# Causal attention with a quantized feed-forward: accumulators of P·V per slot, one score bank per slot, and softmax steps in another order on VectorE

## The chip, the cores and the metric

The kernel runs on all 8 cores of one Trainium2 chip, the same program on each with data of its own; the cores exchange nothing. Cores 2b and 2b+1 share batch item b and split its query tiles between them. The time is that of the slowest core in microseconds (us), from device counters. Lower is better.

## The reference

The input `x` is 4 x 4096 x 1024. With `xn = layernorm(x)`:

```python
q, k, v = xn @ Wq.T, xn @ Wk.T, xn @ Wv.T
qk   = (q @ k.T) * C ** (-0.5)          # C = 1024, so 1/32
attn = softmax(where(causal, qk, -inf))
out  = x + attn @ v + (xn @ quantize_int4(kernel) + bias + (xn @ a) @ b)
```

## The kernel before

Every instruction goes through `Plan.op(engine, function, waits, inc)`. The plan keeps one list for each engine, T (TensorE), V (VectorE), S (ScalarE), Y (SyncE, which issues DMAs) and G (GpSimd, which issues DMAs), in the order in which the Python code calls it, and each list is replayed as that engine's queue. So the order of the code is the order of the work: an instruction whose semaphores are not there yet holds up all that stands behind it in its own queue and nothing else. There is no scheduler.

**Stage 1** (to about 460 us) computes K (transposed, to memory) and V (kept in SBUF as `v_res`, bf16) for all 4096 tokens of the batch item, and quantizes the feed-forward weights on VectorE beside it. **Stage 2a** (to about 610 us) computes Q and the feed-forward for the core's own 2048 rows and writes both to memory. The Q projection `e_qproj` accumulates 8 matmuls into one of two banks `psQ`, and ScalarE evicts each bank to `qstage` (L607).

**Stage 2b** (from 631 us) is attention. The 2048 rows are 16 slots of 128 rows. Slot `si` in processing order sees `kcap = 256 * (16 - si)` keys, from 4096 down to 256. Slots go in pairs `k` of an even slot A (`a = 0`) and an odd slot B (`a = 1`). The parts are:

- `e_scores(k)`: the keys come in chunks of 512. For each chunk first A and then B gets a group of 8 matmuls (L809) into a PSUM bank `psS[a][ci % 2]`, two banks for each slot of the pair and four in all. VectorE casts the bank to bf16 `scores` (L821) and takes the maximum of the chunk into `mxcols` (L827, the last chunk after a mask is added, L831 and L835). The next group of the same bank waits for the cast (`sc_prev`). K chunks beyond the first 1024 keys come through a ring of three buffers `kbuf`.
- `e_softmax(si)`: VectorE takes the maximum over the chunks into `mxv` (L855) and scales it by -1/32 into `nbias` (L859). ScalarE takes the exponentials of the row in two halves (L867, L870) with a scale of 1/32, that bias, and row sums into `lsum`. VectorE adds the two sums (L873) and takes the reciprocal into `invl` (L876). `mxv`, `nbias` and `lsum` are single tiles for all slots, so the maximum of B waits for the reciprocal of A.
- `e_trans_av(si)`: for each block of 128 keys a transpose of the probabilities into `psT` (L894), a copy to `ptb` by ScalarE (L900), and two matmuls (L909) into `psAV[0]` and `psAV[1]`, the halves of the 1024 output columns. The transposes run one block ahead. There is one such accumulator; the first matmul of a slot waits for the epilogue of the slot before (`epi_V[si - 1]`).
- `e_epilogue(si)`: VectorE multiplies both halves by `invl` and adds the feed-forward (L928, L931), then adds `x` (L935), and GpSimd's queue stores the result (L940). `e_sdma_fx` loads the feed-forward and `x` tiles, `e_sdma_qt` the query tiles (L755).

The order is written out at the end: after `e_scores(0)`, for each `k`: softmax A, softmax B, scores of pair `k + 1`, product and epilogue of A, product and epilogue of B.

Of the kernel before, what the change touches and what calls it, by code (L numbers as in the profile page):

```python
# [118 lines left out]
def build_nc():  # L119
# [556 lines left out]
    def sb3(n, s, t):  # L676
        return p2b.enter_context(nc.sbuf_tensor(n, s, t))
# [94 lines left out]
    def e_scores(k):  # L772
# [8 lines left out]
        for ci, (off, wdt) in enumerate(chunks):  # L781
# [6 lines left out]
            for a, (jx, kcx, mx_prev) in enumerate(  # L788
# [5 lines left out]
                for dc in range(NCH):  # L794
                    w = []
                    if dc == 0:
                        w.append(v)
                        prev = sc_prev.get((a, ci % 2))
                        if prev is not None:
                            w.append(prev)  # L800
                        if ci == 0:
                            w.append(qt_dma[si])
# [6 lines left out]
                    P.op("T", lambda e, si=si, a=a, ci=ci, dc=dc, wdx=wdx, kap=kap: e.matmul(  # L809
                        psS[a][ci % 2][:, 0:wdx],  # L810
# [8 lines left out]
                if ci == 0 and k >= 2:  # L819
                    wev.append(exp_S.get(2 * (k - 2) + a))  # L820
                ev = P.op("V", lambda e, kp=kp, a=a, ci=ci, off=off, wdx=wdx: e.tensor_copy(  # L821
                    out=scores[kp][a][:, off:off + wdx], in_=psS[a][ci % 2][:, 0:wdx]),
                    waits=wev, inc=chV)
                sc_prev[(a, ci % 2)] = ev
# [25 lines left out]
    def e_softmax(si):  # L850
        a = si % 2
        j = ORDER[si]
        kcap = slot_kcap(j)
        nch = len(score_chunks(kcap))
        v1 = P.op("V", lambda e, a=a, nch=nch: e.reduce_max(  # L855
            mxv[:, :], mxcols[a][:, 0:nch], axis=AX.X),
            waits=[sc_mx_V[si], inv_V.get(si - 1)], inc=chV)
        mx_fin[si] = v1
        v2 = P.op("V", lambda e: e.tensor_scalar(  # L859
            out=nbias[:, :], in0=mxv[:, :], scalar1=-SCALE, scalar2=None, op0=ALU.mult),  # L860
            waits=[v1], inc=chV)
        w = [v2, exp_S.get(si - 1)]
        if si >= 2:
# [5 lines left out]
            bias=nbias[:, 0:1], scale=SCALE, accum_out=lsum[:, 0:1]), waits=w, inc=chS)  # L869
        exp_S[si] = P.op("S", lambda e, kp=kp, a=a, half=half, kcap=kcap: e.activation(  # L870
            out=pbuf[a][:, half:kcap], in_=scores[kp][a][:, half:kcap], func=AF.Exp,
            bias=nbias[:, 0:1], scale=SCALE, accum_out=lsum[:, 1:2]), inc=chS)
# [3 lines left out]
        inv_V[si] = P.op("V", lambda e, si=si: e.reciprocal(  # L876
            out=invl[si % 2][:, :], in_=lsum[:, 0:1]),
            waits=[vsum, epi_V.get(si - 2)], inc=chV)

    def e_trans_av(si):  # L880
# [23 lines left out]
        def em_av(kc):  # L904
            for h in range(2):
                w2 = [ptb_ev[kc]]
                if kc == 0 and h == 0 and si >= 1:
                    w2.append(epi_V.get(si - 1))
                av_lastk[kc] = P.op("T", lambda e, kc=kc, h=h, nk=nk: e.matmul(  # L909
                    psAV[h][:, :], ptb[kc % 3][:, :],  # L910
                    v_res[:, kc * C + h * 512: kc * C + (h + 1) * 512],
                    start=(kc == 0), stop=(kc == nk - 1), skip_group_check=True),
                    waits=w2, inc=chT)
# [9 lines left out]
    def e_epilogue(si):  # L923
        j = ORDER[si]
        w = [av_T[si], inv_V[si], ff_dma[si], xr_dma[si]]
        if si >= 2:
            w.append(out_G[si - 2])
        P.op("V", lambda e, si=si: e.scalar_tensor_tensor(  # L928
            out=outsb[si % 2][:, 0:512], in0=psAV[0][:, :], scalar=invl[si % 2][:, 0:1],
            in1=fftile[si % 3][:, 0:512], op0=ALU.mult, op1=ALU.add), waits=w, inc=chV)  # L930
        v2 = P.op("V", lambda e, si=si: e.scalar_tensor_tensor(  # L931
            out=outsb[si % 2][:, 512:1024], in0=psAV[1][:, :], scalar=invl[si % 2][:, 0:1],
# [124 lines left out]
```

How the kernel before makes its waits and increments, by code:

```python
    def replay(self, eng, engobj, sems):  # L102
        for ws, fn, semname, amt in self.items[eng]:
            seen = set()
            for n, v in ws:
                key = n
                if key in seen:
                    v = max(v, dict(ws).get(n, v))
                    continue
                seen.add(key)
                vv = max(val for (nn, val) in ws if nn == n)
                engobj.wait_ge(sems[n], vv)
            ins = fn(engobj)
            if semname is not None:
                ins.then_inc(sems[semname], amt)
```

## Time and profile before

| | us |
|---|---|
| median of 2 runs | 1031.19 (1031.08 to 1031.31) |
| the profiled execution's own time | 1031.55 |
| span of its slowest core (core 2), first to last instruction | 1030.0 |
| spans of the eight cores | 1016.6 to 1030.0 |
| TensorE matmuls busy, of the span | 754.1 (73%) |
| VectorE busy | 473.7 (46%) |
| ScalarE busy | 271.7 (26%) |
| mean granted TensorE clock of core 2, share of full speed | 0.887 |

Busy shares are means over stages with different limits. The profile also gives for each instruction its start, its duration and what it waited for; "idle before" is the time that its engine stood still just before it, with the instruction that ended the wait. Some matmul records are missing from a trace (a few per cent). The granted clock is 1.00 at 2.4 GHz and 0.50 at 1.2 GHz, and a value between is a mean over a stretch.

### The profile page before, as it was taken

What the parts mean: (1) busy time and instruction counts of PE and PEld (TensorE: products, weight loads), DVE (VectorE), ACT (ScalarE), POOL (GpSimd) and SP (SyncE); (2) the same over time, 40 slices, a digit from 0 to 9 for tenths busy, and PEclk for the clock granted to TensorE, in tenths of its full rate; (3) what the DMA queues carried; (4) which work ended last, traced back from release to release, by engine and by line L of the source; (5) the groups of instructions that cost most, each with busy time, mean ns of one, the idle gap of its engine ahead of it and who ended that gap; (6) DMA issues with size and microseconds to landing.
All of it is one profiled execution on the core that took longest, in us unless ns stands there. A gap on an engine that the chain in (4) does not pass through costs nothing.

```text
span 1030.0 us, 12140 instructions; the slowest of 8 cores (1016.6 to 1030.0 us)
## 1 busy us (share of the span) xinstructions
PE 754.1 (73%) x3129; PEld 319.7 (31%) x3191; DVE 473.7 (46%) x798; ACT 271.7 (26%) x617; POOL 41.0 (4%) x70
## 2 busy tenths in 40 slices
PE   0055988998998995157989764698878787788752
PEld 0001333343333442012434332344434343333320
DVE  1236467686685695063363322661161331522442
ACT  0023333433333331123121100113413324233321
POOL 2000000000000001000000000000001001011110
PEclk9997999899999998578989886899988898888985
DMA  8970031422403102920421239743243043033232
GB/s 178 215 102 1 41 54 49 103 28 76 102 11 92 56 7 80 158 34 41 122 84 82 82 127 302 266 131 115 102 167 120 21 164 124 21 123 121 82 133 95
DMA packets 35316, 103.32 MB, mean 100 GB/s; under 512 B 2706, under 2 KB 15252, under 8 KB 30772
## 3 DMA queue, kind: packets, MB, share of 16 engines
q0 software_dynamic: 22720, 44.11, 19.9%
q1 hardware_dynamic: 12532, 58.43, 15.7%
q8 instruction: 31, 0.51, 0.2%
q14 instruction: 33, 0.27, 0.1%
HBM read 92.11 MB, written 29.36 MB: 118 GB/s over the span
## 4 chain that ended last, share of the span: by engine, by line
PE 56%; DVE 16%; issue 12%; DMA 9%; ACT 5%; DVEq 1%; SPq 0%; ACTq 0%; POOLq 0%; POOL 0%
PE psAV L909 15%; PE psK L366 9%; PE psS L809 9%; PE psV L393 5%; PE psQ L601 5%; PE psF L631 4%; DMA w<-wker 4%; DMA xga<-xcols 2%; DMA qtile<-qT_h 2%; PE psT L894 2%; ACT pbuf L867 1%; ACT pbuf L870 1%; DVE outsb L935 1%; DVE outsb L928 1%; DVE xg L346 1%
## 5 line engine op out<-in xcount | busy, mean ns | idle before, releaser
L909 PE MATMUL psAV<-v_res,ptb 128*128 128x512 bf16 x527 | 161.4, 411 | 45.7 <-DVE outsb L935 25.4
L393 PE MATMUL psV<-wvb,xg 128*128 128x512 bf16 x504 | 115.8, 387 | 14.4 <-ACT v_res L403 14.0
L900 ACT COPY ptb<-psT 128x128 bf16<-128x128 bf16 x272 | 70.4, 265 | 198.6 <-PE psT L894 196.4
L366 PE MATMUL psK<-xg,wkb 128*128 128x512 bf16 x497 | 113.0, 383 | 5.3 <-ACT kst L372 2.9
L809 PE MATMUL psS<-kbuf,qtile 128*128 128x512 bf16 (+1 forms) x330 | 78.6, 402 | 21.2 <-DVE scores L821 20.9
L909 PEld LDWEIGHTS psAV<-v_res,ptb 128*128 128x128 bf16 x544 | 53.6, 102 | 117.1 <-issue 98.2
L928 DVE SCALAR_TENSOR_TENSOR outsb<-psAV,invl,fft 128x512 f32<-128x512 f32 x16 | 12.0, 750 | 162.9 <-PE psT L894 71.5
L809 PE MATMUL psS<-k_res,qtile 128*128 128x512 bf16 (+1 forms) x236 | 55.9, 396 | 30.0 <-DMA qtile<-qT_h 29.7
L393 PEld LDWEIGHTS psV<-wvb,xg 128*128 128x128 bf16 x512 | 50.3, 99 | 78.8 <-issue 23.8
L366 PEld LDWEIGHTS psK<-xg,wkb 128*128 128x128 bf16 x512 | 50.3, 99 | 66.7 <-issue 8.0
L894 PE MATMUL psT<-identb_s,pbuf 128*128 128x128 bf16 x272 | 59.8, 230 | 6.6 <-ACT pbuf L867 6.4
L631 PE MATMUL psF<-weff,xga 128*128 128x512 bf16 x251 | 58.8, 391 | 7.9 <-DVE ffst L645 7.5
L821 DVE CAST scores<-psS 128x512 bf16<-128x512 f32 x72 | 47.4, 658 | 33.8 <-PE psS L809 33.4
L601 PE MATMUL psQ<-xga,wqb 128*128 128x512 bf16 x249 | 57.5, 387 | 3.6 <-ACT qst L607 2.9
L372 ACT CAST kst<-psK 128x512 bf16<-128x512 f32 x64 | 37.3, 585 | 69.5 <-PE psK L366 69.5
L809 PEld LDWEIGHTS psS<-kbuf,qtile 128*128 128x128 bf16 x336 | 35.3, 106 | 65.3 <-issue 35.6
L288 ACT ACTIVATE sq<-xg 128x512 bf16<-128x512 bf16 x64 | 38.5, 626 | 40.6 <-PE T L298 38.6
L530 PE MATMUL U<-xga,onescol_s 128*1 128x512 bf16 x32 | 16.7, 523 | 43.1 <-ACT sqa L524 32.9
L867 ACT ACTIVATE pbuf<-scores,nbias 128x2048 bf16<-128x2048 bf16 (+15 forms) x16 | 19.2, 1201 | 108.4 <-DVE nbias L859 90.9
L809 PEld LDWEIGHTS psS<-k_res,qtile 128*128 128x128 bf16 x240 | 24.0, 102 | 61.4 <-issue 39.0
L294 PE MATMUL T<-xg,onescol_s 128*1 128x512 bf16 x64 | 32.8, 512 | 12.7 <-DVE rbc_s L334 11.1
L827 DVE TENSOR_REDUCE mxcols<-scores 128x1 f32<-128x512 bf16 x56 | 38.4, 686 | 5.8
(102 smaller groups left out, 755.1 us busy)
## 6 DMA issues: line engine op xcount, KB each, us to landing
kbuf<-kT_h SPq DMA_DIRECT2D x21, 1024.0 KB, 6.7
w<-wker SPq DMA_DIRECT2D x16, 512.0 KB, 6.9
xg<-xfm POOLq DMA_DIRECT2D x8, 1024.0 KB, 11.7
kT_h<-kst SPq DMA_DIRECT2D x8, 1024.0 KB, 3.8
ff_h<-ffst SPq DMA_DIRECT2D x16, 512.0 KB, 2.7
fft<-ff_h POOLq DMA_DIRECT2D x16, 512.0 KB, 6.2
xrt<-xrows POOLq DMA_DIRECT2D x16, 512.0 KB, 7.2
out<-outsb POOLq DMA_DIRECT2D x16, 512.0 KB, 2.9
```

Source lines behind the costliest of these rows:

```text
L288: sq_S[(g, cc)] = P.op("S", lambda e, g=g, cc=cc: e.activation(out=sqb[cc % 2][:, :], in_=xg[g % 3][:, cc * G1:(cc + 1) * G1], func=AF.Squ ...
L366: P.op("T", lambda e, g=g, dc=dc, cc=cc: e.matmul(psK[dc % 2][:, :], wkb[:, :].rearrange("p (a x) -> p a x", a=NCH)[:, cc, dc * 128:(dc + ...
L372: ev[dc] = P.op("S", lambda e, g=g, dc=dc: e.copy(out=kstage[g % 2][:, dc * G1:(dc + 1) * G1], in_=psK[dc % 2][:, :]), waits=[tmm] + ([kst ...
L393: P.op("T", lambda e, g=g, tt=tt, h=h, cc=cc: e.matmul(psV[tt % 2][h][:, :], xg[g % 3][:, cc * G1 + tt * 128: cc * G1 + (tt + 1) * 128], w ...
L601: P.op("T", lambda e, b=b, dc=dc, cc=cc: e.matmul(psQ[dc % 2][:, :], wqb[:, :].rearrange("p (a x) -> p a x", a=NCH)[:, cc, dc * 128:(dc + ...
L631: P.op("T", lambda e, b=b, tt=tt, h=h, cc=cc: e.matmul(psF[tt % 2][h][:, :], xga[b % 3][:, cc * G1 + tt * 128: cc * G1 + (tt + 1) * 128], ...
L809: P.op("T", lambda e, si=si, a=a, ci=ci, dc=dc, wdx=wdx, kap=kap: e.matmul(psS[a][ci % 2][:, 0:wdx], qtile[si % 4][:, dc * 128:(dc + 1) * ...
L821: ev = P.op("V", lambda e, kp=kp, a=a, ci=ci, off=off, wdx=wdx: e.tensor_copy(out=scores[kp][a][:, off:off + wdx], in_=psS[a][ci % 2][:, 0 ...
L827: P.op("V", lambda e, kp=kp, a=a, ci=ci, off=off, wdx=wdx: e.reduce_max(mxcols[a][:, ci:ci + 1], scores[kp][a][:, off:off + wdx], axis=AX. ...
L894: tt = P.op("T", lambda e, a=a, kc=kc: e.transpose(psT_[kc % 2][:, :], pbuf[a][:, kc * 128:(kc + 1) * 128], identb[:, :]), waits=w, inc=chT)
L900: ptb_ev[kc] = P.op("S", lambda e, kc=kc: e.copy(out=ptb[kc % 3][:, :], in_=psT_[kc % 2][:, :]), waits=wv, inc=chS)
L909: av_lastk[kc] = P.op("T", lambda e, kc=kc, h=h, nk=nk: e.matmul(psAV[h][:, :], ptb[kc % 3][:, :], v_res[:, kc * C + h * 512: kc * C + (h ...
```

## The change

The change touches four things.

1. The 16 halves of PSUM used in stage 2b are dealt out anew: `psAV` becomes two accumulators of two banks, chosen by the parity of the slot, and `psS` becomes one bank for each slot of a pair instead of two. The first P·V matmul of a slot waits for the epilogue of the slot two before, and each score group waits for the cast of the group before it in the same slot.
2. `e_softmax` is split. `e_sm_pre` has the maximum and the exponentials, `e_sm_post` the sum and the reciprocal. The scores of the next pair now stand between the two.
3. The factor 1/32 moves from the softmax to the eviction of Q. The maximum is taken with its sign changed, straight into `nbias`, and the separate scaling on VectorE is gone. The maximum of B waits for the exponentials of A, because `nbias` is still one tile.
4. `lsum` has two columns for each slot of a pair.

```diff
-            ev[dc] = P.op("S", lambda e, b=b, dc=dc: e.copy(
+            ev[dc] = P.op("S", lambda e, b=b, dc=dc: e.activation(
                 out=qstage[b % 2][:, :].rearrange(
                     "p (o a t) -> p o a t", o=4, a=NCH)[:, :, dc, :],
-                in_=psQ[dc % 2][:, :].rearrange("p (o t) -> p o t", o=4)),
+                in_=psQ[dc % 2][:, :].rearrange("p (o t) -> p o t", o=4),
+                func=AF.Copy, scale=SCALE),
...
-    lsum = sb3("lsum", [128, 2], F32)
+    lsum = sb3("lsum", [128, 4], F32)
...
-    psS = [[ps3(f"psS{a}_{i}", [128, 512]) for i in range(2)] for a in range(2)]
+    psS = [ps3(f"psS{a}", [128, 512]) for a in range(2)]
     psT_ = [ps3(f"psT{i}", [128, 128], BF16) for i in range(2)]
-    psAV = [ps3(f"psAV_{h}", [128, 512]) for h in range(2)]
+    psAV = [[ps3(f"psAV{i}_{h}", [128, 512]) for h in range(2)] for i in range(2)]
...
-                        prev = sc_prev.get((a, ci % 2))
+                        prev = sc_prev.get(a)
...
-                sc_prev[(a, ci % 2)] = ev
+                sc_prev[a] = ev
...
-    def e_softmax(si):
+    def e_sm_pre(si):
...
         v1 = P.op("V", lambda e, a=a, nch=nch: e.reduce_max(
-            mxv[:, :], mxcols[a][:, 0:nch], axis=AX.X),
-            waits=[sc_mx_V[si], inv_V.get(si - 1)], inc=chV)
+            nbias[:, :], mxcols[a][:, 0:nch], axis=AX.X, negate=True),
+            waits=[sc_mx_V[si], exp_S.get(si - 1)], inc=chV)
         mx_fin[si] = v1
-        v2 = P.op("V", lambda e: e.tensor_scalar(
-            out=nbias[:, :], in0=mxv[:, :], scalar1=-SCALE, scalar2=None, op0=ALU.mult),
-            waits=[v1], inc=chV)
-        w = [v2, exp_S.get(si - 1)]
+        w = [v1, exp_S.get(si - 1)]
...
-            bias=nbias[:, 0:1], scale=SCALE, accum_out=lsum[:, 0:1]), waits=w, inc=chS)
+            bias=nbias[:, 0:1], scale=1.0, accum_out=lsum[:, 2 * a:2 * a + 1]), waits=w, inc=chS)
...
-        vsum = P.op("V", lambda e: e.tensor_tensor(
-            out=lsum[:, 0:1], in0=lsum[:, 0:1], in1=lsum[:, 1:2], op=ALU.add),
+
+    def e_sm_post(si):
+        a = si % 2
+        vsum = P.op("V", lambda e, a=a: e.tensor_tensor(
+            out=lsum[:, 2 * a:2 * a + 1], in0=lsum[:, 2 * a:2 * a + 1],
+            in1=lsum[:, 2 * a + 1:2 * a + 2], op=ALU.add),
             waits=[exp_S[si], inv_V.get(si - 1)], inc=chV)
...
-                if kc == 0 and h == 0 and si >= 1:
-                    w2.append(epi_V.get(si - 1))
+                if kc == 0 and h == 0 and si >= 2:
+                    w2.append(epi_V.get(si - 2))
...
-                    psAV[h][:, :], ptb[kc % 3][:, :],
+                    psAV[si % 2][h][:, :], ptb[kc % 3][:, :],
...
     for k in range(NP2):
-        e_softmax(2 * k)
-        e_softmax(2 * k + 1)
+        e_sm_pre(2 * k)
+        e_sm_pre(2 * k + 1)
         if k + 1 < NP2:
             e_sdma_qt(k + 1)
             e_scores(k + 1)
+        e_sm_post(2 * k)
+        e_sm_post(2 * k + 1)
```

On VectorE, in the cycle of pair 1, from the last epilogue of pair 0 to the first casts of the scores of pair 2, before the change (`psS0_0` is the first bank of the even slot, `psS0_1` its second):

```order
L935 TENSOR_TENSOR outsb1<-outsb1,xrt1 128x1024
L855 TENSOR_REDUCE mxv<-mxcols0 128x1
L859 TENSOR_SCALAR nbias<-mxv 128x1
L873 TENSOR_TENSOR lsum<-lsum 128x1
L876 RECIPROCAL invl0<-lsum 128x1
L855 TENSOR_REDUCE mxv<-mxcols1 128x1
L859 TENSOR_SCALAR nbias<-mxv 128x1
L873 TENSOR_TENSOR lsum<-lsum 128x1
L876 RECIPROCAL invl1<-lsum 128x1
L821 CAST scores0_0<-psS0_0 128x512
L827 TENSOR_REDUCE mxcols0<-scores0_0 128x1
L821 CAST scores0_1<-psS1_0 128x512
```

and the same place after the change:

```order
L936 TENSOR_TENSOR outsb1<-outsb1,xrt1 128x1024
L855 TENSOR_REDUCE nbias<-mxcols0 128x1
L855 TENSOR_REDUCE nbias<-mxcols1 128x1
L822 CAST scores0_0<-psS0 128x512
L828 TENSOR_REDUCE mxcols0<-scores0_0 128x1
L822 CAST scores0_1<-psS1 128x512
```

Six of the eight small operations between the epilogue and the first cast are gone from there: two no longer exist, and four stand behind the scores.

On VectorE again, at the end of the scores of pair 2 in that cycle, after the change, with the four moved operations:

```order
L836 TENSOR_REDUCE mxcols1<-scores0_1 128x1
L873 TENSOR_TENSOR lsum<-lsum 128x1
L877 RECIPROCAL invl0<-lsum 128x1
L873 TENSOR_TENSOR lsum<-lsum 128x1
L877 RECIPROCAL invl1<-lsum 128x1
L929 SCALAR_TENSOR_TENSOR outsb0<-psAV0_0,invl0,fft2 128x512
L932 SCALAR_TENSOR_TENSOR outsb0<-psAV0_1,invl0,fft2 128x512
```

The epilogue of the even slot, which needs `invl0`, comes right behind them, as before it came right behind the scores.

On TensorE the order of the work is the same, and only the banks differ. The first score groups of pair 1 before:

```order
L809 MATMUL psS0_0<-k_res,qtile2 128x512 x8
L809 MATMUL psS1_0<-k_res,qtile3 128x512 x8
L809 MATMUL psS0_1<-k_res,qtile2 128x512 x8
L809 MATMUL psS1_1<-k_res,qtile3 128x512 x8
L809 MATMUL psS0_0<-kbuf0,qtile2 128x512 x8
```

and after:

```order
L810 MATMUL psS0<-k_res,qtile2 128x512 x8
L810 MATMUL psS1<-k_res,qtile3 128x512 x8
L810 MATMUL psS0<-k_res,qtile2 128x512 x8
L810 MATMUL psS1<-k_res,qtile3 128x512 x8
L810 MATMUL psS0<-kbuf0,qtile2 128x512 x8
```

A bank comes round again in the fifth group before, and in the third after.

## Rows read from the trace of the kernel before

**Rows 1.** The head of the page, before

```profile
span 1030.0 us, 12140 instructions; the slowest of 8 cores (1016.6 to 1030.0 us)
```

**Rows 2.** Waits of TensorE from 631 us on: total us, times, longest

```profile
PE psS L809 <- DMA qtile<-qT_h: 29.7, 2, 21.1
PE psAV L909 <- DVE outsb L935: 25.4, 8, 3.5
PE psS L809 <- DVE scores L821: 20.9, 4, 6.4
```

**Rows 3.** Timeline of VectorE, cycle of pair 1: start, us, what, [idle before <- releaser]

```profile
737.57 0.75 DVE L928 SCALAR_TENSOR_TENSOR outsb<-psAV,invl,fft 128x512 f32<-128x512 f32 x1 [19.85 <-PE psAV L909]
...
744.66 0.16 DVE L873 TENSOR_TENSOR lsum<-lsum 128x1 f32<-128x1 f32 x1 [4.03 <-ACT pbuf L870]
...
745.19 0.16 DVE L855 TENSOR_REDUCE mxv<-mxcols 128x1 f32<-128x7 f32 x1
...
749.43 0.16 DVE L873 TENSOR_TENSOR lsum<-lsum 128x1 f32<-128x1 f32 x1 [3.81 <-ACT pbuf L870]
...
749.93 0.69 DVE L821 CAST scores<-psS 128x512 bf16<-128x512 f32 x1
```

**Rows 4.** Timeline of TensorE: restart of the scores, even slot, odd slot

```profile
750.77 15.48 PE L809 MATMUL psS<-kbuf,qtile 128*128 128x512 bf16 x63 [6.43 <-DVE scores L821]
...
766.96 0.59 PE L909 MATMUL psAV<-v_res,ptb 128*128 128x512 bf16 x2 [0.61 <-ACT ptb L900]
...
787.31 1.01 PE L909 MATMUL psAV<-v_res,ptb 128*128 128x512 bf16 x2 [3.16 <-DVE outsb L935]
```

**Rows 5.** Timeline of VectorE, two casts in the steady part of the scores

```profile
762.02 0.69 DVE L821 CAST scores<-psS 128x512 bf16<-128x512 f32 x1 [0.25 <-PE psS L809]
...
763.75 0.69 DVE L821 CAST scores<-psS 128x512 bf16<-128x512 f32 x1 [0.25 <-PE psS L809]
```

**Rows 6.** Chain behind an odd slot's start: start, us, what

```profile
789.39 0.85 PE psAV L909 x2
...
790.35 0.85 PE psAV L909 x2
...
798.60 0.59 PE psAV L909 x2
...
799.81 0.59 PE psAV L909 x2
```

**Rows 7.** Windows, columns: length, PE, PEld, DVE, ACT, POOL busy, granted clock, DMA, GB/s

```profile
717.30:737.40 20.10, 18.30 (x87) 8.94 (x90) 0.42 (x1) 7.42 (x28) 2.65 (x5) 0.92 0.38 131
786.50:804.60 18.10, 16.58 (x73) 7.77 (x75) 0.66 (x1) 6.36 (x24) 2.66 (x5) 0.82 0.43 145
849.00:864.50 15.50, 14.42 (x63) 6.76 (x65) 0.00 (x0) 5.30 (x20) 2.66 (x5) 0.82 0.47 171
902.00:913.50 11.50, 10.91 (x50) 5.03 (x49) 0.00 (x0) 4.17 (x16) 2.28 (x5) 0.85 0.61 229
943.00:952.00 9.00, 8.55 (x37) 3.94 (x38) 0.00 (x0) 3.04 (x12) 2.66 (x5) 0.81 0.77 274
750.80:767.00 16.20, 15.54 (x66) 6.99 (x67) 13.79 (x22) 0.43 (x2) 0.00 (x0) 0.85 0.46 147
```

**Rows 8.** Timeline of the cycle of pair 5: TensorE and VectorE

```profile
952.86 6.21 PE L809 MATMUL psS<-k_res,qtile 128*128 128x512 bf16 x32
...
958.65 0.16 DVE L873 TENSOR_TENSOR lsum<-lsum 128x1 f32<-128x1 f32 x1 [2.32 <-ACT pbuf L870]
...
962.19 0.38 PE L909 MATMUL psAV<-v_res,ptb 128*128 128x512 bf16 x1 [3.00 <-DVE invl L876]
```

**Rows 9.** Groups by line, ScalarE: count, busy us, mean ns, idle before

```profile
L288 ACT ACTIVATE sq<-xg 128x512 bf16<-128x512 bf16 x64 | 38.5, 626 | 40.6 <-PE T L298 38.6 <-PE T L294 1.5
...
L607 ACT CAST qst<-psQ 128x512 bf16<-128x512 f32 x32 | 18.6, 584 | 79.8 <-PE psQ L601 79.8
...
L288 ACT ACT_TABLE_LOAD x1 | 1.3, 1283 | 58.9 <-DMA xg<-xfm 58.9
```

More of the change, by code:

```diff
@@ L808, in e_scores @@
                             :, dc, 0:wdx]
-                    P.op("T", lambda e, si=si, a=a, ci=ci, dc=dc, wdx=wdx, kap=kap: e.matmul(
-                        psS[a][ci % 2][:, 0:wdx],
+                    P.op("T", lambda e, si=si, a=a, dc=dc, wdx=wdx, kap=kap: e.matmul(
+                        psS[a][:, 0:wdx],
                         qtile[si % 4][:, dc * 128:(dc + 1) * 128],
@@ L820, in e_scores @@
                     wev.append(exp_S.get(2 * (k - 2) + a))
-                ev = P.op("V", lambda e, kp=kp, a=a, ci=ci, off=off, wdx=wdx: e.tensor_copy(
-                    out=scores[kp][a][:, off:off + wdx], in_=psS[a][ci % 2][:, 0:wdx]),
+                ev = P.op("V", lambda e, kp=kp, a=a, off=off, wdx=wdx: e.tensor_copy(
+                    out=scores[kp][a][:, off:off + wdx], in_=psS[a][:, 0:wdx]),
                     waits=wev, inc=chV)
-                sc_prev[(a, ci % 2)] = ev
+                sc_prev[a] = ev
                 nchx = nchA if a == 0 else nchB
@@ L848, in e_scores @@
         qt_cons[2 * k + 1] = sc_fin_T[k]
-    def e_softmax(si):
+    def e_sm_pre(si):
         a = si % 2
-        j = ORDER[si]
-        kcap = slot_kcap(j)
+        kcap = slot_kcap(ORDER[si])
         nch = len(score_chunks(kcap))
         v1 = P.op("V", lambda e, a=a, nch=nch: e.reduce_max(
-            mxv[:, :], mxcols[a][:, 0:nch], axis=AX.X),
-            waits=[sc_mx_V[si], inv_V.get(si - 1)], inc=chV)
+            nbias[:, :], mxcols[a][:, 0:nch], axis=AX.X, negate=True),
+            waits=[sc_mx_V[si], exp_S.get(si - 1)], inc=chV)
         mx_fin[si] = v1
-        v2 = P.op("V", lambda e: e.tensor_scalar(
-            out=nbias[:, :], in0=mxv[:, :], scalar1=-SCALE, scalar2=None, op0=ALU.mult),
-            waits=[v1], inc=chV)
-        w = [v2, exp_S.get(si - 1)]
+        w = [v1, exp_S.get(si - 1)]
         if si >= 2:
@@ L868, in e_softmax @@
             out=pbuf[a][:, 0:half], in_=scores[kp][a][:, 0:half], func=AF.Exp,
-            bias=nbias[:, 0:1], scale=SCALE, accum_out=lsum[:, 0:1]), waits=w, inc=chS)
+            bias=nbias[:, 0:1], scale=1.0, accum_out=lsum[:, 2 * a:2 * a + 1]), waits=w, inc=chS)
         exp_S[si] = P.op("S", lambda e, kp=kp, a=a, half=half, kcap=kcap: e.activation(
             out=pbuf[a][:, half:kcap], in_=scores[kp][a][:, half:kcap], func=AF.Exp,
-            bias=nbias[:, 0:1], scale=SCALE, accum_out=lsum[:, 1:2]), inc=chS)
-        vsum = P.op("V", lambda e: e.tensor_tensor(
-            out=lsum[:, 0:1], in0=lsum[:, 0:1], in1=lsum[:, 1:2], op=ALU.add),
+            bias=nbias[:, 0:1], scale=1.0, accum_out=lsum[:, 2 * a + 1:2 * a + 2]), inc=chS)
+    def e_sm_post(si):
[3 more added lines that the diff above has]
+            in1=lsum[:, 2 * a + 1:2 * a + 2], op=ALU.add),
             waits=[exp_S[si], inv_V.get(si - 1)], inc=chV)
-        inv_V[si] = P.op("V", lambda e, si=si: e.reciprocal(
-            out=invl[si % 2][:, :], in_=lsum[:, 0:1]),
+        inv_V[si] = P.op("V", lambda e, si=si, a=a: e.reciprocal(
+            out=invl[si % 2][:, :], in_=lsum[:, 2 * a:2 * a + 1]),
             waits=[vsum, epi_V.get(si - 2)], inc=chV)
@@ L906, in em_av @@
                 w2 = [ptb_ev[kc]]
-                if kc == 0 and h == 0 and si >= 1:
-                    w2.append(epi_V.get(si - 1))
-                av_lastk[kc] = P.op("T", lambda e, kc=kc, h=h, nk=nk: e.matmul(
-                    psAV[h][:, :], ptb[kc % 3][:, :],
+                if kc == 0 and h == 0 and si >= 2:
+                    w2.append(epi_V.get(si - 2))
+                av_lastk[kc] = P.op("T", lambda e, si=si, kc=kc, h=h, nk=nk: e.matmul(
+                    psAV[si % 2][h][:, :], ptb[kc % 3][:, :],
                     v_res[:, kc * C + h * 512: kc * C + (h + 1) * 512],
@@ L928, in e_epilogue @@
         P.op("V", lambda e, si=si: e.scalar_tensor_tensor(
-            out=outsb[si % 2][:, 0:512], in0=psAV[0][:, :], scalar=invl[si % 2][:, 0:1],
+            out=outsb[si % 2][:, 0:512], in0=psAV[si % 2][0][:, :], scalar=invl[si % 2][:, 0:1],
             in1=fftile[si % 3][:, 0:512], op0=ALU.mult, op1=ALU.add), waits=w, inc=chV)
         v2 = P.op("V", lambda e, si=si: e.scalar_tensor_tensor(
-            out=outsb[si % 2][:, 512:1024], in0=psAV[1][:, :], scalar=invl[si % 2][:, 0:1],
+            out=outsb[si % 2][:, 512:1024], in0=psAV[si % 2][1][:, :], scalar=invl[si % 2][:, 0:1],
             in1=fftile[si % 3][:, 512:1024], op0=ALU.mult, op1=ALU.add), inc=chV)
```

## Prediction

> **What bounds the kernel now.** I read the page's head first: the eight cores lie between 1016.6 and 1030.0 us, and the page is that of the slowest [rows 1]. They run the same program on data of their own, so one core's chain decides. The change is in the attention stage (631 us to the end), apart from one eviction. There I read who TensorE waited for. Three entries count [rows 2]: 29.7 us for the first query tiles, which the change does not touch; 25.4 us in 8 waits of the P·V product on the epilogue's last addition (L935); and 20.9 us in 4 waits of the scores on the cast that empties a score bank (L821). The last two are what is aimed at.
>
> The timeline of one cycle shows how they arise. A cycle is one pair of slots: two P·V products, the scores of the next pair between them. In VectorE's queue [rows 3] the epilogue of the odd slot starts at 737.57; then come maximum and bias. At 744.66 `lsum` has waited 4.03 us for the first slot's two exponentials (A). Four small operations later the second slot's exponentials (B) may start, and at 749.43 VectorE comes out of the wait for them too. Only then, at 749.93, does it cast the first score bank. TensorE had filled its four banks and stood for 6.43 us, until 750.77 [rows 4]. The other wait is the row at 787.31: 3.16 us idle, because both slots of a pair use one P·V accumulator and the epilogue of the even slot must read it first.
>
> **Separate P·V accumulators.** The odd slot now waits for the epilogue two slots back, which is long past. What is late next is the hand-over of the first transposed block: where the wait is absent (the even slot at 766.96) TensorE idles 0.61 us for it [rows 4]. So each wait is worth 25.4 / 8 = 3.18 less 0.6, and 8 x 2.6 = 20.6 us. The last of them gives less: slot 15 has one pair of key blocks, shorter than the epilogue of slot 14, behind which its own epilogue then queues; I take off 0.6. **Term 1: 20.0 us.** The cover is the P·V product of the odd slot, at least 3.6 us (6 blocks at 0.6) for slots 1 to 13 against an epilogue of 2.7 us.
>
> **VectorE's queue and the banks of the scores.** In the cycle shown, that of pair 1, of the small operations, spaced 0.26 us (744.66 to 745.19 is two of them [rows 3]), six of eight leave this place: the two scalings are gone, the two sums and two reciprocals stand behind the scores. After the change: one operation less ahead of A, so A's end is seen at 744.66 - 0.26 = 744.40; the maximum of B (0.26); the cast at about 744.67; and, as now, TensorE 0.84 us behind the start of the cast (749.93 to 750.77), at 745.5. That is 5.3 us earlier. But with one bank per slot TensorE has done two groups of eight matmuls by then and not four. A group is 1.73 us, the spacing of casts in the steady part [rows 5], so 3.45 us of work is left over. Net gain 1.8 us, and the wait before the cast stays, at some 4.7 us instead of 6.4. VectorE must still wait for A, since both slots share one bias tile: behind that wait stand the maximum of B and all casts, and TensorE waits for these.
>
> B shrinks as slots get shorter. `lsum` waited 4.03 us at 3584 keys and 2.32 us at 1536 [rows 3, 8], four cycles later, so 0.43 us less a cycle. The four cycles that stall now give 1.8, 1.4, 1.0 and 0.5 us. In the cycle of pair 5 (1536 keys) the next scores are four groups, which now fit the four banks; TensorE's wait is behind B, since the copies of the transposed blocks stand in ScalarE's queue after it (3.00 us before 962.19 [rows 8]). The scores there begin at 952.86 and A is seen done at 958.65 [rows 8], after the change 5.5 us in; the maximum (0.26) and the cast with its hand-over (0.84) follow, so with two banks TensorE goes on at 6.6. The last 2.6 us of score work and the entry of the product (two transposes 0.3, idle 0.6 as at 766.96) put the P·V product at 10.1 us, where it now starts at 9.3. That loses 0.8. In the two last cycles at most two groups are left, no bank is short, and B starts four small operations earlier: 1.0 each. **Term 2: 1.8 + 1.4 + 1.0 + 0.5 - 0.8 + 1.0 + 1.0 = 5.9 us.** The trace shows no kernel with one bank per slot. From below, all four stalls could stay as long as they are with two groups less done (4 x 3.45 = 14 us lost); from above they could lose B's whole share (4 x 5.3 = 21 us gained). I stand near the row-by-row value, since each of its steps has a row.
>
> **The clock.** After each wait the granted clock is at its lower level, 1.2 GHz instead of 2.4, for a while. Behind 787.31 a block takes 0.96 us (789.39 to 790.35); later two take 1.21 (798.60 to 799.81, one between them) [rows 6]. The five products that follow a long epilogue wait ran at mean clocks of 0.92, 0.82, 0.82, 0.85 and 0.81 [rows 7]. Twice the missing share times the stretch is the time at the lower level: 3.2, 6.5, 5.6, 3.5 and 3.4 us, together 22.2. In that time 1 - 0.60/0.96 = 37.5% is lost: 8.3 us, and about 1 us for the short odd slots after them. Without the wait TensorE goes on with its work, so I expect this back. **Term 3: 9.3 us**, from nothing (the clock falls there anyway) to 9.3. The score stalls have their own price: 0.85 over 16.2 us behind the restart at 750.8 [rows 7] is 4.9 us at the lower level, 2.4 us lost. Those stalls stay over 3 us, as long as the epilogue waits that now suffice for a fall, so I leave the price as it is, with bounds of 5 us gained (shorter falls in all four) and 3 us lost (one more fall in the cycle of pair 5 and longer ones elsewhere).
>
> **The eviction of Q.** It becomes an activation with a constant scale. The cast takes 584 ns; an activation of the same 512 columns elsewhere takes 626 [rows 9], so 32 x 0.04 = 1.3 us of ScalarE, beside groups of 1.73 us with two banks: nothing. If it needed its own table each time (one load in this trace, 1.28 us), 0.63 + 1.28 would exceed 1.73 by 0.18, 32 times: 6 us at most. The exponentials without their scale keep their length. The sums moved behind the scores wait for nothing: B ends long before the scores do, and the epilogue that needs them comes after a whole P·V product. In the last cycle there are no scores, and they stand where they stood. SP's and POOL's queues keep their order.
>
> **Sum.** 20.0 + 5.9 + 9.3 = 35.2 us. The profiled execution took 1031.55 us (span 1030.0); 1031.55 - 35.2 = 996.4. The median of the runs is 0.4 lower, so 996.0 us.
>
> **Rivals.**
> 1. *The clock does not come back.* Score stalls and ends of slots remain, and the clock falls as often as now. For it: a wait of 3.16 us is enough for a fall, and the stalls that stay are longer. Against it: the falls in rows 7 each sit behind a wait that goes. Terms 1 and 2 only: 1031.2 - 25.9 = 1005.3 us.
> 2. *The wait returns as a wait for a transfer.* TensorE reaches the scores sooner, and key, query or feed-forward tiles are late. For it: the query tiles cost 29.7 us at the start [rows 2]. Against it: behind a restart the scores run at the pace they have now, so key tiles have the lead they have now, and no row shows TensorE waiting for them. All of terms 1 and 3 gone: 1025.3 us, within 2%.
> 3. *Slower: the scores fall to the low clock.* With one bank per slot each group needs the cast of the group before last. The cast begins about 0.25 us after the matmuls and takes 0.69, and TensorE follows 0.15 later: 1.1 us, against 1.73 us of the other slot's group. That hides, by 0.6 us. Should it not, TensorE would pause in every group, and if these pauses held the clock at its lower level a group would take 3.45 us. The 56 groups after the first pair, seven of them half as wide, are 52.5 full groups: 52.5 x 1.73 = 91 us more, 996 + 91 = 1087 us. It decides from a hand-over of 1.73 us on, and turns the sum to slower than 2% once pauses cost 56 us, 1.0 us a group. Rows 5 speak against it: VectorE is idle 0.25 us in each group, so the cast is not queued.
> The Trainium skill has this rule against the change ("TensorE: Matmul & The Clock Gate", section "A second HAM failure mode: psum-queue depth-cycling"): cycling through PSUM banks leaves short idle moments between groups, often enough for the clock to swing. By that rule the time would be near rival 3's; in this trace four banks are cycled in the scores, and the casts come evenly 1.73 us apart at full clock, which does not bear it out for four, while no row shows two.
> 4. *The change does not shorten VectorE's queue,* because casts stay behind B. The order shows them ahead of the sums, and ScalarE alone runs B. Then the four stalls cost 3.45 more each and their gain of 4.7 is gone: 996 + 14 + 5 = 1015 us, with an own spread of 5 to either side.
>
> **How the numbers follow.** Forecast 0.75, rival 1 0.13, rival 2 0.04, rival 3 0.03, rival 4 0.05. The range runs from 987 (term 2 and the clock of the stalls better by 9) to 1008 (rival 1 and 3 us of new falls). A measurement of this kernel tells 2%, some 21 us, from no change: faster means under 1010.6. The forecast and rival 1 are faster, 0.88; rival 4 straddles the bound, and about half of it counts there too: 0.91. Within 2% are rival 2 and its other half, 0.06. Slower is rival 3, 0.03.
>
> **What would show it.** Right: TensorE's waits on the epilogue's addition are gone; its waits on the casts are still there, five and not four, 3 to 5 us each; no fall of the clock at the start of an odd slot; the casts of a long slot 1.73 us apart; span near 995. Term 1 is wrong if the odd slots begin with another wait; term 3 if the mean clock of an odd slot's product stays near 0.85; term 2 if the waits on casts sum to over 30 us. Regular idle of TensorE between score groups would make the whole forecast wrong.

## Result and profile after

The changed kernel takes 994.17 us (median) against 1031.28 us for the kernel before in the same series: the ratio is 0.9642, 95% interval 0.9631 to 0.9653. The forecast was 996.0. In most series some executions ran at a lower granted clock on part of the cores and took up to 9% longer; the medians of this document count them, the ratios and their intervals leave them out, so the ratios are what to compare. The head of its page and TensorE's waits from 631 us on (total us, times, longest), to be read against [rows 1, 2]:

```profile
span 992.0 us, 12186 instructions; the slowest of 8 cores (981.9 to 992.0 us)
```

```profile
PE psS L810 <- DMA qtile<-qT_h: 29.6, 2, 22.1
PE psS L810 <- DVE scores L822: 19.2, 5, 4.5
PE psAV L910 <- ACT ptb L901: 11.6, 18, 2.4
PE psT L895 <- ACT pbuf L864: 5.9, 2, 4.2
PE psAV L910 <- DVE lsum L873: 2.0, 1, 2.0
```

The 25.4 us of waits on the epilogue's last addition are gone. The hand-over of the transposed blocks took their place under its own name (ScalarE's copy L901): 11.6 us in 18 waits, where it was 3.6 us in 8. The waits of the scores on the casts are still there in total, 19.2 us instead of 20.9, but five of them instead of four. The timeline of VectorE in the cycle of pair 1, against [rows 3]:

```profile
733.55 0.75 DVE L929 SCALAR_TENSOR_TENSOR outsb<-psAV,invl,fft 128x512 f32<-128x512 f32 x1 [15.85 <-PE psAV L910]
...
736.20 0.15 DVE L855 TENSOR_REDUCE nbias<-mxcols 128x1 f32<-128x7 f32 x1
740.32 0.16 DVE L855 TENSOR_REDUCE nbias<-mxcols 128x1 f32<-128x7 f32 x1 [3.96 <-ACT pbuf L867]
740.56 0.69 DVE L822 CAST scores<-psS 128x512 bf16<-128x512 f32 x1
...
753.71 0.69 DVE L822 CAST scores<-psS 128x512 bf16<-128x512 f32 x1 [0.25 <-PE psS L810]
...
755.44 0.69 DVE L822 CAST scores<-psS 128x512 bf16<-128x512 f32 x1 [0.25 <-PE psS L810]
```

From the first operation of the epilogue to the cast it is 7.01 us, against 12.36 before (737.57 to 749.93). The one long wait left is the second row: VectorE stands 3.96 us for the exponentials of A, since these still read the bias tile that the maximum of B is to overwrite. Further down two casts are 1.73 us apart with VectorE idle 0.25 us before each, as in [rows 5], so the single bank holds nobody up in the steady part. On TensorE, against [rows 4], the start of an odd slot, the restart of the scores of that cycle, and then the cycle of pair 5, against [rows 8]:

```profile
715.24 0.59 PE L910 MATMUL psAV<-v_res,ptb 128*128 128x512 bf16 x2 [0.50 <-ACT ptb L901]
...
741.40 5.30 PE L810 MATMUL psS<-k_res,qtile 128*128 128x512 bf16 x16 [4.53 <-DVE scores L822]
```

```profile
923.24 3.61 PE L810 MATMUL psS<-k_res,qtile 128*128 128x512 bf16 x16
929.78 4.44 PE L810 MATMUL psS<-k_res,qtile 128*128 128x512 bf16 x16 [2.93 <-DVE scores L822]
...
934.98 0.59 PE L910 MATMUL psAV<-v_res,ptb 128*128 128x512 bf16 x2 [0.65 <-ACT ptb L901]
```

This odd slot, the first, starts after 0.50 us of idle; before the change it waited 3.10 us, and the odd slot of [rows 4] 3.16. The clock, in windows of the products of slots 1, 3 and 5 and then behind the restart at 741.4, against [rows 7]; the number before the last two is the granted clock:

```profile
715.20:731.50 16.30, 15.38 (x82) 7.62 (x82) 2.39 (x3) 6.96 (x27) 2.65 (x5) 1.00 0.48 162
778.10:792.00 13.90, 13.09 (x70) 6.65 (x70) 2.36 (x3) 5.83 (x22) 2.67 (x5) 1.00 0.51 189
832.00:846.00 14.00, 12.71 (x68) 6.31 (x67) 2.64 (x3) 5.74 (x22) 2.66 (x5) 1.00 0.55 189
741.40:760.40 19.00, 18.39 (x83) 8.41 (x83) 13.94 (x21) 3.16 (x6) 0.00 (x0) 0.91 0.38 138
```

These odd slots run at the full 2.4 GHz, as do the other five (1.00 in each), and the falls of the clock that are left in this stage sit behind the score stalls.

**Where the time went, interval by interval.** Each slot has one epilogue, and the starts of its first operation (L928, L929 after the change) cut the attention stage into 15 intervals. Eight run from an even slot's epilogue to its odd slot's and hold the wait on the accumulator. Seven run from an odd slot's to that of the next even slot and hold the exponentials, the score stall and the scores. In us, read from VectorE's timeline:

| | even to odd (8) | sum | odd to even (7) | sum |
|---|---|---|---|---|
| before | 22.59 21.18 18.71 15.42 13.02 9.17 8.43 5.13 | 113.7 | 46.85 40.40 33.54 26.57 16.27 14.90 11.12 | 189.7 |
| after | 18.59 16.24 13.83 11.42 9.05 6.63 4.20 2.66 | 82.6 | 44.28 38.75 31.77 24.75 18.88 13.90 10.36 | 182.7 |

So 31.0 us came from the first kind and 7.0 us from the second. I use the same two sums for the experiments. They are of the slowest core of one execution each, so a difference of some 1 us between two sums says nothing. Where one core could mislead, the mean over the eight cores of the execution is given beside it: 113.1 and 189.1 us before, 83.0 and 182.2 after.

### The profile page after: what moved, and what is told of

It reads as the page before. It is cut to its first block, busy times and chain, and to the rows that moved or that the text cites. A ratio compares the mean times of both kernels' runs of the same rounds, so it can differ in the third digit from the quotient of the medians.

```text
span 992.0 us, 12186 instructions; the slowest of 8 cores (981.9 to 992.0 us)
## 1 busy us (share of the span) xinstructions
PE 746.5 (75%) x3191; PEld 316.0 (32%) x3191; DVE 472.0 (48%) x782; ACT 272.2 (27%) x617; POOL 41.0 (4%) x70
## 4 chain that ended last, share of the span: by engine, by line
PE 62%; DVE 13%; DMA 10%; issue 9%; ACT 5%; DVEq 0%; SPq 0%; ACTq 0%; POOLq 0%; POOL 0%
PE psAV L910 14%; PE psS L810 12%; PE psK L366 10%; PE psV L393 6%; PE psQ L601 5%; PE psF L632 5%; DMA w<-wker 4%; DMA xga<-xcols 2%; DMA qtile<-qT_h 2%; PE T L298 2%; PE T L294 2%; PE psT L895 1%; PE U L534 1%; DVE ab_sb L251 1%; PE T L325 1%
## 5 line engine op out<-in xcount | busy, mean ns | idle before, releaser
L910 PE MATMUL psAV<-v_res,ptb 128*128 128x512 bf16 x544 | 152.2, 385 | 20.1 <-ACT ptb L901 11.6
L901 ACT COPY ptb<-psT 128x128 bf16<-128x128 bf16 x272 | 70.4, 265 | 170.7 <-PE psT L895 168.4
L810 PE MATMUL psS<-k_res,qtile 128*128 128x512 bf16 (+1 forms) x240 | 65.9, 441 | 49.0 <-DMA qtile<-qT_h 29.6
L929 DVE SCALAR_TENSOR_TENSOR outsb<-psAV,invl,fft 128x512 f32<-128x512 f32 x16 | 12.0, 751 | 133.1 <-PE psT L895 72.3
L810 PE MATMUL psS<-kbuf,qtile 128*128 128x512 bf16 (+1 forms) x336 | 68.4, 364 | 0.0
L895 PE MATMUL psT<-identb_s,pbuf 128*128 128x128 bf16 x272 | 57.5, 221 | 5.9 <-ACT pbuf L864 5.9
L810 PEld LDWEIGHTS psS<-k_res,qtile 128*128 128x128 bf16 x240 | 26.0, 112 | 88.4 <-issue 72.2
L864 ACT ACTIVATE pbuf<-scores,nbias 128x2048 bf16<-128x2048 bf16 (+15 forms) x16 | 19.2, 1201 | 100.3 <-DVE nbias L855 78.9
L810 PEld LDWEIGHTS psS<-kbuf,qtile 128*128 128x128 bf16 x336 | 32.9, 98 | 35.8
```

Of the source, the lines that this page charges most:

```text
L810: P.op("T", lambda e, si=si, a=a, dc=dc, wdx=wdx, kap=kap: e.matmul(psS[a][:, 0:wdx], qtile[si % 4][:, dc * 128:(dc + 1) * 128], kap, star ...
L895: tt = P.op("T", lambda e, a=a, kc=kc: e.transpose(psT_[kc % 2][:, :], pbuf[a][:, kc * 128:(kc + 1) * 128], identb[:, :]), waits=w, inc=chT)
L901: ptb_ev[kc] = P.op("S", lambda e, kc=kc: e.copy(out=ptb[kc % 3][:, :], in_=psT_[kc % 2][:, :]), waits=wv, inc=chS)
L910: av_lastk[kc] = P.op("T", lambda e, si=si, kc=kc, h=h, nk=nk: e.matmul(psAV[si % 2][h][:, :], ptb[kc % 3][:, :], v_res[:, kc * C + h * 51 ...
```

## Experiments

Each experiment was timed in a series with the kernel before, which took 1029.1 us for the first four, 1032.4 for the next four and 1030.9 for the last, so ratios are what can be compared across.

### Order alone, banks alone

The order alone is the changed kernel with the banks put back; the index of a bank changes with them wherever it is used. It keeps the softmax in two parts, the four columns of `lsum` and the scaling of Q, so "order" below stands for all three (the scaling has an experiment of its own).

```diff
-    psS = [ps3(f"psS{a}", [128, 512]) for a in range(2)]
-    psAV = [[ps3(f"psAV{i}_{h}", [128, 512]) for h in range(2)] for i in range(2)]
+    psS = [[ps3(f"psS{a}_{i}", [128, 512]) for i in range(2)] for a in range(2)]
+    psAV = [ps3(f"psAV_{h}", [128, 512]) for h in range(2)]
...
-                if kc == 0 and h == 0 and si >= 2:
-                    w2.append(epi_V.get(si - 2))
+                if kc == 0 and h == 0 and si >= 1:
+                    w2.append(epi_V.get(si - 1))
```

Expected: 

> The changed kernel with the PSUM banks dealt out as before (two score banks per slot, one P.V accumulator, its wait on the epilogue of the slot before). By the steps of the prediction, but with four groups done when the first cast comes: the four score stalls shrink from 20.9 us to about 3 (restart 5.3, 4.8, 4.4, 4.0 us earlier and nothing given back), three late cycles gain 1.0 each, and the clock behind those stalls comes back, 8 to 11 us; the 8 waits on the epilogue stay at 25 us. Together 29 to 33 us: 998 to 1002 us. A rival theory, that the gain of the change comes from the separate accumulators and the queue's order is worth only its term of 5.9 us, gives 1025 us.

Measured: 998.36 us, ratio 0.969 (0.9658 to 0.9722). TensorE's waits in it:

```profile
PE psAV L910 <- DVE outsb L936: 25.2, 8, 3.2
...
PE psS L810 <- DVE scores L822: 2.5, 3, 1.1
```

The casts come as early as in the changed kernel, but four banks hold TensorE's work until then: 2.5 us of stall instead of 20.9. The sums are 111.8 and 156.7 us: 33 us of gain lie in the second kind of interval, 2 in the first, where the waits on the accumulator are all there. The rival (order worth 5.9 us) is out.

The banks alone are the same pieces the other way round: the new banks and the new wait, put into the kernel before. Expected: 

> The kernel before with only the banks changed (one per slot for scores, two P.V accumulators), VectorE's order, the scaling and the single sum tile as before. Terms 1 and 3 of the prediction are gained, 29.3 us; the four score stalls do their restart at the same time as before but with two groups done instead of four, 4 x 3.45 = 14 us lost, and up to 5 more with the clock and the cycle of pair 5: 1016 to 1021 us, with waits on the casts of about 35 us. A rival, that one bank per slot also costs in the steady part of the scores, gives 1030 us and more, with regular idle of TensorE between groups.

Measured: 1017.44 us, ratio 0.988 (0.9841 to 0.992). The waits on the casts, the cycle of pair 1 on TensorE, and the restart in the cycle of pair 5:

```profile
PE psS L809 <- DVE scores L821: 41.3, 5, 9.8
```

```profile
731.64 3.61 PE L809 MATMUL psS<-k_res,qtile 128*128 128x512 bf16 x16
745.09 6.51 PE L809 MATMUL psS<-k_res,qtile 128*128 128x512 bf16 x16 [9.84 <-DVE scores L821]
751.44 13.12 PE L809 MATMUL psS<-kbuf,qtile 128*128 128x512 bf16 x64
...
951.65 4.78 PE L809 MATMUL psS<-k_res,qtile 128*128 128x512 bf16 x16 [6.53 <-DVE scores L821]
```

Two groups, then 9.84 us of idle where it was 6.43: 3.41 us more, and the two groups that no longer fit are 3.45. The four long cycles together wait 34.8 us, the 35 expected; the fifth wait, 6.53 us in the cycle of pair 5, was in the expected time only within the "up to 5 more". Behind the restart 64 matmuls follow in one piece of 13.12 us, so one bank per slot costs nothing that shows in the steady part. The sums are 82.8 and 207.6 us: 31 gained in the first kind, 18 lost in the second (14 expected from the four stalls and up to 5 more).

So the change is not a sum of two gains. Banks alone give 1.2%, order alone 3.1%, together 3.6%. The new banks take two score banks away, and that costs most of what they give as long as VectorE comes late to the casts.

### The accumulator's wait, put back whole and in part

The separate accumulators stay, and only the awaited token is changed.

```diff
-                if kc == 0 and h == 0 and si >= 2:
-                    w2.append(epi_V.get(si - 2))
+                if kc == 0 and h == 0 and si >= 1:
+                    w2.append(epi_V.get(si - 1))
```

Expected: 

> The changed kernel, with the first P.V matmul of a slot again waiting for the whole epilogue of the slot before, although the accumulators are separate. This puts back terms 1 and 3 alone: 994.2 + 20 + 9.3 = 1023.5 us, with the granted clock of the odd slots' products back at 0.82 to 0.92. If the clock would fall anyway (rival 1), only the wait comes back: 1014 us.

Measured: 1020.81 us, ratio 0.9913 (0.9883 to 0.9944), 2.7% above the changed kernel's ratio, 28 us. The sums are 112.7 and 182.6 us, so all of it, 30.1 us, is in the first kind of interval. That is terms 1 and 3 measured directly (29.3 in the prediction), and it rules out the 1014 us that a clock falling anyway would give.

For the second kernel the same line appends `ff_cons.get(si - 1)`, the second operation of the epilogue. Expected: 

> The changed kernel, with the first P.V matmul of a slot waiting for the second operation of the epilogue of the slot before (the last that reads the accumulator), not the third. Each wait is then 3.16 - 1.1 = 2.0 us and costs 1.4 beyond the hand-over: 11 us. If a wait of 2 us no longer drops the clock the time is 994.2 + 11 = 1005 us; if it still does, 1005 + 9.3 = 1014 us.

Measured: 1004.33 us, ratio 0.9741 (0.9703 to 0.9778). Its wait is 14.5 us in 8 pieces, and the sums are 97.2 and 182.4, 14.6 us more than in the changed kernel in the first kind. By the ratios it is 1.0% above the changed kernel, 10 us, with the intervals 6 to 14. That alone would pass for a clock that does not fall (11 us expected, against 20), but the profile shows a mixture: the clock fell in part of the slots. Against the changed kernel the eight intervals are longer by 2.66, 2.68, 2.68, 1.24, 2.56, 1.21, 1.22 and 0.31. There are two sizes: 1.2 is the wait beyond the hand-over, and what the larger ones have on top, 1.3 to 1.5 us, is the clock. The mean over the eight cores is 95.1 us, 12.1 more than in the changed kernel, with the larger size in 19 of the 56 intervals of slots 1 to 13. Windows of the products of slots 1, 3, 5 and 7 show it:

```profile
712.20:730.00 17.80, 16.98 (x82) 8.28 (x83) 1.19 (x1) 7.03 (x27) 2.65 (x5) 0.90 0.44 148
778.20:795.00 16.80, 15.99 (x76) 7.67 (x76) 1.19 (x1) 6.36 (x24) 2.66 (x5) 0.90 0.43 157
836.00:850.00 14.00, 13.31 (x62) 6.35 (x62) 1.23 (x1) 5.30 (x20) 2.66 (x5) 0.88 0.50 190
884.50:895.50 11.00, 9.71 (x51) 4.86 (x52) 1.83 (x2) 4.24 (x16) 2.67 (x5) 1.00 0.61 233
```

On this core a wait of 1.8 us was followed by the lower level four times (slots 1, 3, 5 and 9) and four times not. Even in the kernel with the whole wait back, one slot kept its clock behind 3.15 us, the second of these windows:

```profile
714.40:732.00 17.60, 16.77 (x81) 8.17 (x81) 0.00 (x0) 6.93 (x26) 2.65 (x5) 0.90 0.42 150
781.30:796.00 14.70, 13.88 (x74) 6.90 (x74) 0.00 (x0) 6.31 (x24) 2.66 (x5) 1.00 0.49 179
```

The kernel before has such a slot too, slot 11, which [rows 7] leave out:

```profile
972.41 0.59 PE L909 MATMUL psAV<-v_res,ptb 128*128 128x512 bf16 x2 [3.14 <-DVE outsb L935]
```

```profile
972.41:978.70 6.29, 5.95 (x29) 2.78 (x31) 0.00 (x1) 2.12 (x8) 2.67 (x5) 1.00 0.70 249
```

### The wait that is left: two bias tiles

```diff
-    nbias = sb3("nbias", [128, 1], F32)
+    nbias = [sb3(f"nbias{i}", [128, 1], F32) for i in range(2)]
...
-            nbias[:, :], mxcols[a][:, 0:nch], axis=AX.X, negate=True),
-            waits=[sc_mx_V[si], exp_S.get(si - 1)], inc=chV)
+            nbias[a][:, :], mxcols[a][:, 0:nch], axis=AX.X, negate=True),
+            waits=[sc_mx_V[si], exp_S.get(si - 2)], inc=chV)
```

Expected: 

> The changed kernel with two bias tiles, one for each slot of a pair, so that VectorE no longer waits for the exponentials of A before it takes the maximum of B and casts. The theory of the change (what is left in the score stalls is that wait) says: the five waits on casts (19.2 us) shrink to what the epilogue and two small operations take beyond two groups, 0.4 + 2.7 + 0.5 + 0.8 - 3.45 = 1 us or less each, some 15 us gained, and the clock behind them comes back, about 8 us: 968 to 973 us. A rival, that one score bank per slot or the copies behind B would hold TensorE as long anyway, gives 988 us or more, with the waits under other names.

Measured: 966.83 us, ratio 0.9364 (0.9346 to 0.9383). The score stalls, and the restart in the cycle of pair 1:

```profile
PE psS L810 <- DVE scores L822: 1.9, 5, 0.5
```

```profile
738.06 2.10 PE L810 MATMUL psS<-k_res,qtile 128*128 128x512 bf16 x9 [0.30 <-DVE scores L822]
```

The 19.2 us are 1.9, and the sums are 83.2 and 154.8: all 28 us come from the second kind of interval. It is a little more than the 21 to 26 us expected. The mean granted clock from 700 to 900 us, with the changed kernel first and this one second:

```profile
700.00:900.00 200.00, 174.06 (x843) 81.34 (x842) 68.28 (x115) 73.13 (x223) 12.79 (x24) 0.96 0.32 114
```

```profile
700.00:900.00 200.00, 186.74 (x950) 89.62 (x949) 75.96 (x131) 80.82 (x253) 15.44 (x29) 1.00 0.34 122
```

The same edit on the order alone asks what the separate accumulators are worth once nobody waits for casts. Expected: 

> The kernel with only the order changed (banks as before), and two bias tiles. Its score stalls were 2.5 us in all, so little is left there: 994 to 997 us against 998. This says what the separate accumulators are worth once the stalls at the casts are gone: 968 to 973 us (two bias tiles with the new banks) is lower by terms 1 and 3, 25 to 29 us. If the gains of banks and order overlap as in the changed kernel (4 us between order alone and all), the difference is 5 us or less.

Measured: 992.99 us, ratio 0.962 (0.9592 to 0.9648), with sums of 112.9 and 152.2. So with two bias tiles the new banks give 2.6% (0.962 to 0.9364), where without them they gave 0.5% (0.969 to 0.9642). The casts are then early enough for two banks. Two bias tiles with the old order were not run.

| | banks as before | new banks |
|---|---|---|
| order as before | 1 | 0.988 |
| new order | 0.969 | 0.9642 |
| new order, two bias tiles | 0.962 | 0.9364 |

### The scaling put back

The factor 1/32 goes back to VectorE and to the exponential, and Q is evicted by a plain copy. Expected: 

> The changed kernel with the factor 1/32 back in the softmax (a scaling on VectorE after each maximum, plain copies of Q). Two operations of 0.26 us return to the chain between epilogue and cast of seven cycles: 7 x 0.52 = 3.6 us, 998 us. If they are hidden: 994 us.

Measured: 996.99 us, ratio 0.9656 (0.9637 to 0.9675), whose interval overlaps that of the changed kernel. The second sum is 187.9, 5.3 us more than without: 0.4 to 0.5 in three of the intervals, 0.1 to 0.2 in two, and 1.9 and 1.6 in the other two, more than two small operations can take. The other seven cores do not show that much: their second sums are 182.5 to 184.8, and the mean over the eight is 184.6, 2.4 us more than in the changed kernel. The sign and the place are as expected; the size is 1.4 us by the ratios and 2.4 by this mean, not apart from nothing in the timed runs, and under the 3.6 worked out. Evicting Q by activation costs 595 ns on average instead of 584 [rows 9], with no further table load.

### Beyond the change

With two bias tiles, the two maxima are moved right behind the scores, ahead of the epilogues:

```diff
             e_scores(k + 1)
+            e_bias(2 * k + 2)
+            e_bias(2 * k + 3)
         e_sm_post(2 * k)
```

Expected: 

> As the kernel with two bias tiles, and the two maxima stand right behind the scores in VectorE's queue, ahead of the epilogues; the exponentials then need nothing of VectorE at the start of a cycle. The remaining stalls of the long cycles shrink by another 0.3 to 0.5 us each, and the cycles of pairs 5, 6 and 7, whose P.V product waits for the exponentials, begin them about 3 us earlier: 9 to 11 us less than with two bias tiles alone, 958 to 963 us. If the copies of the slot before, in ScalarE's queue, are what holds the exponentials, nothing more is gained.

Measured: 960.51 us, ratio 0.9302 (0.9283 to 0.932), the fastest kernel of the study, 7% below the kernel before. The sums are 83.6 and 147.7, so 7.1 us less, nearly all in the last two cycles (12.90 to 8.48 and 9.69 to 7.45). It is less than the 9 to 11 expected: the cycle of pair 5 gained 0.3 and not 3, since its product waits for the scores there. It starts 0.76 us behind the end of their last group, 0.65 of it idle for the hand-over:

```profile
905.41 2.76 PE L810 MATMUL psS<-k_res,qtile 128*128 128x512 bf16 x16 [0.28 <-DVE scores L822]
...
908.93 0.59 PE L913 MATMUL psAV<-v_res,ptb 128*128 128x512 bf16 x2 [0.65 <-ACT ptb L904]
```

And in the last two epilogues VectorE met transfers:

```profile
DVE outsb L932 <- DMA xrt<-xrows: 3.8, 1, 3.8
...
DVE outsb L932 <- DMA out<-outsb: 1.2, 1, 1.2
```

The last kernel moves the loads of the even slot ahead of a store in GpSimd's queue:

```diff
         e_trans_av(2 * k)
+        if k + 1 < NP2:
+            e_sdma_fx(k + 1, (0,))
         e_epilogue(2 * k)
         if k + 1 < NP2:
-            e_sdma_fx(k + 1)
+            e_sdma_fx(k + 1, (1,))
```

Expected: 

> As the kernel with the early maxima, and the loads for the even slot of the next pair stand ahead of the store of the even slot in GpSimd's queue. In the kernel with the early maxima the epilogue of slot 14 waited 3.8 us for its load of x and that of slot 15 another 1.2 us for a store. The loads of slot 14 now start one epilogue and one store earlier, some 8 us. If these waits set the end, 3 to 5 us go: 956 to 958 us, ratio 0.926 against 0.930. If only their names change (a store waits behind the load), 960 us.

Measured: 960.57 us, ratio 0.9323 (0.9304 to 0.9341): no gain that these runs can show. The wait on the load is gone in its profile and the last interval of the second kind fell from 7.45 to 3.99 us, but the waits for the stores grew from 1.2 us to 1.7:

```profile
DVE outsb L932 <- DMA out<-outsb: 1.7, 1, 1.7
```

On other cores of the same execution these waits add up to 1.4 to 4.2 us. The stage as a whole is 2.9 us shorter in the one profiled execution (228.4 against 231.2 us from the first epilogue to the last, and as much in the mean over the cores), which the timed runs don't bear out. In the profiled executions the first epilogue came 2.9 us later in the mean over the cores (713.3 against 710.4 us), and the edit touches nothing ahead of it; whether that is chance is open.

## Why the prediction was right

996.0 us was forecast and 994.17 measured: 35.2 us of gain against 37.1, with 38.0 in the stage by the two profiles.

- **Terms 1 and 3**, 29.3 us together, measured 31.0 between the profiles and 30.1 by putting the wait back. Their parts can be told apart too. In the sixth interval of the kernel before and in the second of the one with the wait restored, the clock stayed at 1.00, and the difference to the changed kernel is 2.54 and 2.56 us, which is the 2.6 that I took for the wait beyond the hand-over. The rest is term 3: 1.4 to 2.4 us in each of the intervals of slots 1 to 9, some 11 us in all, a little more than the 9.3. So the sentence that the clock is at its lower level after each wait is wrong for slot 11 of the kernel before, on this core; the sum did not suffer, since it priced the five slots before it by their own rows. The deduction for slot 15 fits (2.47 us, clock and all).
- **Term 2**, 5.9 us, measured 7.0, with two errors in it that cancel in part. The restart of pair 1 is right to 0.1: from the start of the scores it came after 13.50 us before (737.27 to 750.77) and comes after 8.15 now (733.25 to 741.40), 5.35 us earlier where 5.3 was worked out. In all four long cycles the restarts came 5.35, 4.92, 4.13 and 4.06 us earlier, less 3.45 each 4.7 us, as worked out. But these cycles gained 7.8 us, since the clock behind the shorter stalls was better than I had left it. From restart to product it was 0.84, 0.76, 0.68 and 0.50 before and 0.91, 0.82, 0.85 and 0.81 after, which is 6.5 us less at the lower level, or 3.2 us of work. The last of the four, before and after (the first window ends 0.6 us into the product):

```profile
924.30:930.00 5.70, 5.49 (x18) 2.54 (x18) 5.22 (x9) 0.17 (x2) 0.00 (x0) 0.53 0.00 0
```

```profile
896.41:903.83 7.42, 7.42 (x33) 3.47 (x34) 5.30 (x8) 1.45 (x4) 0.00 (x0) 0.81 0.01 2
```

The prediction had put this share at nothing, with bounds of 5 us gained and 3 lost. The two last cycles gained 1.0 and 0.8.
- **The cycle of pair 5** lost 2.6 us and not 0.8. Its restart came 6.54 us into the cycle, as worked out (6.6), but the last two score groups took 4.44 us instead of 2.6, since the clock fell behind the new stall (0.60 over the 4.28 us to the product). The product started 11.7 us in, not 10.1. I had named this fall as a bound and not as the likely case. On three of the eight cores the clock stayed at 1.00 there and the cycle lost 1.0 us, close to the 0.8; on these the cycle before it was 1.5 us longer instead. That these two errors of term 2, a gain of 2.9 us and a loss of 1.8, nearly cancel is luck.
- **Rivals.** Rival 1 (the clock does not come back) is refuted by the windows at 1.00 and by the restored wait. Rival 2 (transfers) did not come at a size that counts: on the slowest core no wait for a transfer took the place of the others, and on two other cores the last epilogue waited 1.7 and 0.6 us for a store. On the slowest core such waits reach 5.0 us when the stage is 34 us shorter still. Rival 3, the slow scores, and with it the Trainium skill's rule on cycling through PSUM banks ("TensorE: Matmul & The Clock Gate", "A second HAM failure mode: psum-queue depth-cycling"), is not borne out with two banks either: the casts shown above stay 1.73 us apart, and in the kernel with two bias tiles the mean granted clock from 700 to 900 us is 1.00. Rival 4 (casts stay behind B) is ruled out by the timeline.

What the prediction did not see is how the two halves of the change depend on each other. It gave the accumulators 29.3 us and the queue with its banks 5.9. That is right as a division of what was saved by place. As a division by edit it is wrong: the order is worth 32 us alone and the banks 5 us on top of it, or the banks 12 us alone and the order 25 on top.

## What to carry to other kernels

When one edit takes buffers from one wait and gives them to another, work out both waits at the moment when the slowest consumer arrives, and then try each half alone: here the banks gave 12 us alone and 5 us with the new order, and one more tile of 512 bytes, which let the consumer arrive early, raised that to 26 (0.962 to 0.9364). A queue that stands for a result it does not itself need (here the maximum of B, for a tile still being read) is the first thing to look for, since everything behind it waits too. Waits of TensorE of some 3 us cost more here than their length in 14 of 16 cases, and waits of 1.8 us in four of eight, so their price includes the slow stretch behind them.

## What was not expected of the hardware

- The same wait does not always cost the same. Of the 16 waits of 3.05 to 3.51 us on the accumulator in the kernel before and in the one with the wait restored, slowest core of each, two left the clock at 1.00 (slot 11 before, slot 3 restored), and the products behind the others ran at 0.50 to 0.91. Waits of 1.8 us were followed by a fall four times in eight. What decides between the two isn't shown by these runs.
- Stores that land in 2.9 us as a rule (median) took up to 9.0 us at the end of the changed kernel (4.1 before). It is the store of slot 13, issued 1.9 us behind the last of four loads of 512 KB in the same queue; before the change the same store came 5.8 us behind them. No experiment tells the queue from the moment, so the cause is not shown. On one core the epilogue of slot 15 waited 1.7 us for a store. As the cycles got shorter, the last epilogues waited more for transfers: nothing before, up to 1.7 us after the change, and 4.8 to 6.5 us with the early maxima, over the eight cores.
